# A transformer block on one core: the order of work at the joints of the transposed attention

## The reference, cut to what matters

```python
x = L0_attn_hidden_states                  # 2 x 2048 x 256, float32
x = x + 0.5 * ffn(layernorm(x))            # network 1
x = x + attention(layernorm(x))            # complex projections, softmax over 2048 keys
x = x + 0.5 * ffn(layernorm(x))            # network 2
# ffn(x) = fp4(silu(fp4(x) @ fp4(w_gate).T) * (fp4(x) @ fp4(w_up).T)) @ fp4(w_down).T
# fp4: blocks of 16 along the last axis, scale = max|block| / 6, values rounded to a grid of 8
# attention: the scores are the sum over a real and an imaginary part, one softmax for both
```

## Time and profile before

| | us |
|---|---|
| median of 3 runs | 1010.31 (1008.29 to 1010.52) |
| the profiled execution's own time | 1008.92 |
| its span, first to last instruction | 1007.1 |
| PE busy | 934.5 (93% of the span) |
| DVE, ACT, POOL busy | 709.0, 656.7, 505.5 |
| mean granted TensorE clock | 0.981 of full speed |

### The profile page before, as it was taken

The page is one execution under the profiler, slowest core; times in us unless marked ns, Lnnn a source line. Parts: engine busy times, 40 slices in busy tenths (PEclk is TensorE's granted clock), DMA queues, the critical chain, the costliest instruction groups (busy, mean ns, idle before and its releaser), DMA issues.

```text
span 1007.1 us, 18220 instructions
## 1 busy us (share of the span) xinstructions
PE 934.5 (93%) x6607; PEld 870.9 (86%) x6607; DVE 709.0 (70%) x1180; ACT 656.7 (65%) x1380; POOL 505.5 (50%) x593
## 2 busy tenths in 40 slices
PE   3799999999989489999989999999988999999997
PEld 2578888888889489999989999999977888888886
DVE  7889888888757436666555445555575889898996
ACT  5767877888755646666667566666674565555553
POOL 3456667665420074555555535555572565656552
PEclk9999999999999889999999999999999999999998
DMA  9000000000000000000000000000000000000001
GB/s 322 21 1 1 1 2 1 1 1 1 2 1 1 1 1 2 1 2 2 1 2 1 1 2 2 1 1 2 1 2 1 1 22 22 21 22 22 22 1 42
DMA packets 11560, 13.94 MB, mean 14 GB/s; under 512 B 848, under 2 KB 10576, under 8 KB 11472
## 3 DMA queue, kind: packets, MB, share of 16 engines
q1 hardware_dynamic: 11472, 12.79, 3.8%
HBM read 8.59 MB, written 4.19 MB: 13 GB/s over the span
## 4 chain that ended last, share of the span: by engine, by line
PE 65%; DVE 17%; POOL 7%; ACT 5%; issue 4%; DMA 0%; DVEq 0%; SPq 0%; ACTq 0%; POOLq 0%
PE bank L1711 18%; PE bank L1496 14%; POOL zq L487 6%; PE bank L1401 5%; DVE grid L696 3%; DVE amax L668 3%; PE bank_b L1505 3%; DVE rounded L690 3%; PE bank L1759 3%; PE bank_b L1763 3%; PE bank_b L1759 3%; PE bank L1763 3%; PE bank_b L1761 3%; PE bank L1761 3%; DVE z L657 2%
## 5 line engine op out<-in xcount | busy, mean ns | idle before, releaser
L525 POOL TENSOR_TENSOR p_lo<-s_buf,p_hi 128x512 fp32r<-128x512 f32 x128 | 165.0, 1293 | 176.4 <-ACT p_hi L1305 163.5
L487 POOL TENSOR_TENSOR zq<-grid,s_neg 128x64 f32<-128x64 f32 (+2 forms) x188 | 178.0, 971 | 60.3 <-DVE grid L696 50.9
L1496 PE MATMUL bank<-w_hi,T_hi 128*128 128x512 f32 (+1 forms) x384 | 150.1, 391 | 0.7 <-ACT T_lo L1148 0.7
L1711 PE MATMUL bank<-q_hi,k_hi 128*128 128x256 f32 x512 | 145.2, 284 | 1.8 <-DVE q_lo L824 1.8
L1711 PE MATMUL bank<-q_lo,k_hi 128*128 128x256 f32 x512 | 144.9, 283 | 0.0
L1711 PE MATMUL bank<-q_hi,k_lo 128*128 128x256 f32 x512 | 144.8, 283 | 0.0
L1496 PE MATMUL bank<-w_hi,T_lo 128*128 128x512 f32 (+1 forms) x384 | 144.5, 376 | 0.0
L1496 PE MATMUL bank<-w_lo,T_hi 128*128 128x512 f32 (+1 forms) x384 | 144.1, 375 | 0.0
L1290 ACT ACTIVATE s_buf<-bank 128x512 f32<-128x512 f32 x128 | 76.3, 596 | 99.0 <-PE bank L1711 99.0
L849 DVE TENSOR_TENSOR top<-bank,top 128x512 f32<-128x512 f32 x96 | 66.3, 691 | 75.9 <-ACT s_buf L1290 75.9
L1505 PE MATMUL bank_b<-wd_hl,T_hi 128*128 128x256 f32 x744 | 100.0, 283 | 3.0 <-ACT T_hi L1150 2.9
(11 more groups left out here) (202 smaller groups left out, 2541.1 us busy)
## 6 DMA issues: line engine op xcount, KB each, us to landing
out<-x SPq DMA_DIRECT2D x7, 512.0 KB, 2.9
x<-in_L_attn_hidden_states SPq DMA_DIRECT2D x3, 1024.0 KB, 13.9
x<-in_L_attn_hidden_states SPq DMA_DIRECT2D x2, 512.0 KB, 7.9
wraw<-in_L_ffn_w_down SPq DMA_DIRECT2D x1, 704.0 KB, 8.5
wraw<-in_L_ffn_w_gate SPq DMA_DIRECT2D x1, 640.0 KB, 4.6
wraw<-in_L_ffn_w_up SPq DMA_DIRECT2D x1, 640.0 KB, 6.6
wq_s<-in_L_attn_Wq SPq DMA_DIRECT2D x1, 512.0 KB, 8.1
wk_s<-in_L_attn_Wk SPq DMA_DIRECT2D x1, 512.0 KB, 9.5
```

Source lines behind the costliest of these rows:

```text
L487: last = nc.gpsimd.tensor_tensor(out=blocks(zq[:, to:to + hi - lo]), in0=blocks(grid[:, lo:hi]), in1=spread(s_neg[:, par, lo // BLOCK:hi / ...
L525: nc.gpsimd.tensor_tensor(out=p_lo[:, n % 2, 2 * c:2 * c + 2, :], in0=score_buf(n, c), in1=p_hi[:, 2 * c:2 * c + 2, :].bitcast(F32), op=AL ...
L1496: last = nc.tensor.matmul(gu[:, lo:hi], lhsT=T[:, par, HK + kd, :], rhs=w[:, kd, lo:hi], start=n == 0, stop=n == len(terms) - 1)
L1711: last = nc.tensor.matmul(score_bank(c)[:, a, :], lhsT=kk[:, kd, t], rhs=q[:, n % 2, kd, :], start=i == 0 and a == 0, stop=i == len(terms) ...
```

## The change

- **Query bias.** PE does `query_bias` in the first ramp, behind the first transposes of Wo, and ACT's two copies of it stand behind `chain_upper(-3)`. The sum moves to another bank.
- **Exp table.** The load moves from between `evacuate(0, 7)` and `evacuate(1, 0)` to the end of network 1, ahead of `bias_rows`.
- **First group.** On POOL `output_std(7)` moves behind the eight `p_lower(0, c)`. On DVE the shift runs one chunk behind the maximum instead of three.
- **Change of batch.** PE's first transpose of new keys waits for six evacuated chunks instead of eight. `queries(8)` moves from chunk 5 to chunk 2 on PE, and with it its two halves on ACT and DVE; the halves of the keys move one place; ACT's `new_statistics(5)` goes behind the eight exponentials.
- **Last group and ramp.** The first tile of group 15 is summed in `top_bank` instead of `bank_a`. The wait for `x_att` = 32 leaves ACT, and PE has it ahead of `transpose_chain(1, 0)`. On PE the transposes and the gate products of the ramp move forward by one to three chunks of weighted values; on POOL the first `quantised` moves ahead of the last two `p_lower`; on DVE `finish(14)` moves ahead of the scales of the second tile, `finish(15)` behind step -1; on ACT `chain_upper(-4)` goes ahead, and the statistics of group 15 go from step -1 to step 2.

The diff, cut to its core:

```diff
@@ banks
+        def out_bank(n, a):
+            return top_bank if n == NQ - 1 and a == 0 else value_banks[a]
-        bq_sum = bank4[:, 0, 0:1 + KD]
+        bq_sum = bank2[:, 0, 0:1 + KD]
@@ gpsimd
-                    if f == 0 and c % 4 == 1 and c >= 5:
+                    if f == 0 and c % 4 == 1 and 5 <= c < NT:
                         output_std((c - 5) // 4)
...
                 for c in range(CH):
                     p_lower(n - 1, c)
+                if n == 1:
+                    output_std(NG * B - 1)
...
             for c in range(CH):
+                if c == CH - 2:
+                    second_ffn(-5, 1)
                 p_lower(NQ - 1, c)
@@ vector
             running_top(1, 2)
+            shifted(0, 0)
+            shifted(0, 1)
             for c in range(3, CH):
-                shifted(0, c - 3)
                 running_top(1, c)
-            for c in range(CH - 3, CH):
-                shifted(0, c)
+                shifted(0, c - 1)
+            shifted(0, CH - 1)
...
-                if n == NQ - 1:
-                    second_blocks(-5, 1)
+            to_grid(-4)
             finish(NQ - 2)
+            scales(-3, 1)
+            scaled(-3)
             second_blocks(-4, 0)
             second_blocks(-3, 1)
             second_product(0)
             second_ffn(-2, 0)
+            second_ffn(-1, 1)
             finish(NQ - 1)
-            ffn_rounds(second_ffn, -1)
+            ffn_rounds(second_ffn, 0)
@@ scalar
-                    if f and c == -1:
-                        act.wait_ge(x_att, NT)
-                    if f and c == -1:
+                    if f and c == 2:
                         new_statistics(NQ - 1)
                     if extra and c == NT - 1:
+                        nc.scalar.activation(warm[:], mhalf[:, 0:1], ACT.Exp)
                         bias_rows()
...
-                new_statistics(n - 2)
+                if n != HQ - 1:
+                    new_statistics(n - 2)
...
+                if n == HQ - 1:
+                    new_statistics(n - 2)
@@ tensor
+                    if f and c == 0:
+                        pe.wait_ge(x_att, NT)
                     transpose_chain(f, c)
...
                 if n == HQ - 1:
-                    pe.wait_ge(evac_done, CH * (n + 1))
-                    pe.wait_ge(top_done, tops(n, CH - 1))
+                    pe.wait_ge(evac_done, CH * n + 6)
+                    pe.wait_ge(top_done, tops(n, 5))
                     transpose_keys(1, 0)
...
-            weighted_values(n, 0)
             pe.wait_ge(diff_done, CH * NQ)
             transpose_chain(1, -4)
+            weighted_values(n, 0)
+            chain_lower(1, -4, 0)
             weighted_values(n, 1)
-            chain_lower(1, -4, 0)
-            weighted_values(n, 2)
             pe.wait_ge(lo_done, number_lo(1, -4))
             gate_up(0, ((0, 512), (512, 1024), (1024, G))).then_inc(gu_done, 1)
             transpose_chain(1, -3)
+            weighted_values(n, 2)
+            chain_lower(1, -3, 1)
             weighted_values(n, 3)
             weighted_values(n, 4)
-            chain_lower(1, -3, 1)
+            ramp(-2, 0)
             weighted_values(n, 5)
             weighted_values(n, 6)
-            ramp(-2, 0)
+            ramp(-1, 1)
             weighted_values(n, 7)
-            rounds(1, -1)
+            rounds(1, 0)
```

57 lines of the change are left out of this document (28 added, 29 removed).

## The result

| | before | after |
|---|---|---|
| median | 1009.38 (4 runs: 1008.29 to 1010.52) | 984.06 (4 runs: 983.04 to 985.51) |
| the profiled execution's own time | 1008.92 | 983.04 |
| its span | 1007.1 | 981.3 |
| PE busy | 934.5 (93%) | 930.5 (95%) |
| mean granted clock | 0.981 | 0.991 |

The ratio is 0.975, with a 95% interval of 0.9734 to 0.9767: 25.3 us faster by the medians, 25.9 between the two profiled executions. The prediction was 984.0 (980 to 991.5).

What follows compares the result with a forecast made beforehand. The prediction took PE's own work to bound the steady attention, leaving waits and half clock at the joints. Its terms, -2.8 - 17.6 - 2.2 - 2.7 = -25.3 us, gave 983.6 from the profiled run, 985.0 from the median; forecast 984 (980 to 991.5).

Steps and rivals of the forecast that it cites:

- Query bias, -2.8: First ramp and attention's start: moving the one-column passes lets PE start earlier and keep its clock, -2.8 us in sum.
- The block: Attention's start: without the 24 one-column passes PE goes on at 292.4, -1.7 us.
- The clock: Attention's start: half clock from 294.90 to 298.20, put down to the one-column passes, would go: -1.1 us, or 0.
- The table load ahead of `bias_rows`: Attention's start: the Exp load delays ACT's chain by 1.3 us, but costs PE nothing, with +1.3 as other end.
- First group, -17.6: First attention group: shorter ACT rounds, POOL's wait gone and full clock together give -17.6 us.
- (a): First group: earlier shifts on DVE cut ACT's round from 3.13 to 1.78 us, `transpose_top(1)` comes 5.6 us earlier.
- (b): First group: POOL's lower parts no longer wait for tile 31's statistics, so the wait ahead of `weighted_values(0, 0)` goes: -9.6 us.
- (c): First group: half clock behind the two idle times goes, as about 2.5 us of wait remain: -2.4 us, other end 0.
- Change of batch, -2.2: Change of batch: PE's two waits give -1.0 and -1.8 us, ACT's late statistics cost +0.6; bounds -2.8 and 0.
- Last group and ramp, -2.7: Last group to network 2: -2.9 up to tile 0, -1.1 of clock behind it, +1.3 for late statistics; bounds +2 and -4.5.
- so the half clock stays as it was: Last group: PE idles 3.9 us ahead of the first transposes, so the clock loss there was taken as unchanged.
- that rival: First group: DVE's shift and maximum wait for POOL's parts, the round stays long at 4.0 us; 992 us, 8%.

Runs made afterwards that it cites:

- e10_narrow24: Changed kernel with 24 one-column passes (twelve matmuls) put at the attention's start, behind the transposes of the keys: 986.7 us.
- e5_wide: Changed kernel with 22 matmuls of 256 columns put at the attention's start, behind the transposes of the keys: 984.2 us.
- e1_pool: Kernel before with only POOL's first-group edit, `output_std(7)` behind the eight `p_lower(0, c)`: 1000.6 us against 1010.5.
- e2_dve: Kernel before with only DVE's first-group edit, the shift one chunk behind the maximum instead of three: 1001.5 us against 1010.5.
- e12_ramp: `e8_zq4_up` with `chain_rest(-4)` ahead of ACT's Silu table load and PE's last weighted values of group 15 spread between ramp stages: 980.3 us.
- e3_both: Kernel before with POOL's and DVE's first-group edits together, nothing else of the change: 994.2 us against 1010.5.
- e6_split: Changed kernel with the statistics of group 15 split: tile 30 in step 2, tile 31 in step 3 of network 2: 983.9 us.
- e7_zq4: Changed kernel with network 2's first quantised on POOL moved two lower parts earlier, ahead of `p_lower(15, 4)`: 982.5 us.
- e8_zq4_up: `e7_zq4` with ACT's `chain_upper(-4)` also moved, between the upper parts of chunks 6 and 7: 981.8 us.
- e4_narrow: Changed kernel with 12 one-column passes (six matmuls) put at the attention's start, behind the transposes of the keys: 983.0 us.
- e11_evac: Changed kernel with ACT's evacuations of chunks 6 and 7 of group 1 ahead of the exponentials of chunks 3 and 4: 983.8 us.
- e13_all: `e12_ramp` plus `e11_evac`'s order, a later `weighted_values(15, 7)`, statistics of tiles 28 to 31 in steps 0 to 3, DVE's last group-0 shift later: 974.6 us.

## Why the prediction was right

Point by point, by its own steps.

*Query bias, -2.8: right in sum, its two sizes off.* The start gained 2.8 us (2.4 at `scores(0, 0)`, with the first gate products 0.4 us later in the span before anything changed had run). The block is 1.2, not 1.7: `queries(0)` does begin 1.7 us earlier, but 0.4 us go again at the second transposes of keys, for which see the table load below. The clock is 1.6, not 1.1; I had counted matmuls only to 298.20. That the fall hangs on the one-column passes was a guess from one row. `e10_narrow24` against `e5_wide` supports it, but `e1_pool` and `e2_dve` have the passes and no fall: the 1.6 us are what the profiled run of the kernel before had to give, not what every run has. In the first ramp the passes cost nothing, since they lie in the old wait, which ends at 39.15 where it ended at 38.97:

```profile
39.15 0.58 PE L1543 MATMUL bank<-T_hi,neg_ident 128*128 128x256 f32 x1 [2.28 <-ACT T_hi L1152]
```

They saved nothing either: in the first ramp the ledger has 1.6 to 3.0 us in the four kernels with the passes at their old place, and 1.6 to 2.9 in the others (4.8 in `e12_ramp`). So the lower bound of -1.5, the clock kept in this gap, did not come.

The table load ahead of `bias_rows` was put at nothing, and no wait of PE at that place names ACT. But it did cost, by way of DVE:

```profile
293.02 1.06 DVE L647 SCALAR_TENSOR_TENSOR st_junk<-x,nmean,rk_row 128x256 f32<-128x256 f32 x1 [0.27 <-ACT bias_row L1075]
...
298.35 0.47 PE L1700 MATMUL bank<-nv,k_hi 128*128 128x256 f32 x2 [0.18 <-DVE v_hl L842]
```

DVE waited for ACT's row, and then its first statistic ran beside POOL's `bias_row` (293.07, 0.74 us) and took 1.06 us. Before, where POOL was through by then, it was:

```profile
292.28 0.48 DVE L639 SCALAR_TENSOR_TENSOR st_junk<-x,nmean,rk_row 128x256 f32<-128x256 f32 x1
```

From there DVE had no idle time until `v_hl` was done, and PE waited for that at 298.35. From the second transposes of keys to the product behind them PE took 298.35 - 297.13 = 1.22 us, where it took 0.79 before. So the term was about 0.4 us, within its bound of +1.3, but not nothing. This is read from the trace; no run has the load moved alone.

*First group, -17.6: right, -17.8.* (a) -5.8 against -5.6: the round is 1.67 us, a little under my 1.78, since I had left out how far ACT's instructions overlap. (b) -9.6, as read. (c) -2.4, as worked out, but in part by luck. I argued that waits of 1.46 and 1.82 us were not followed by a fall and took 2.5 us for the same kind. Of the nine kernels profiled here with a wait of 2.4 us ahead of `transpose_top(1)` and none behind it, six show a fall behind it, with 1.5 to 1.7 us lost (`e3_both`, `e6_split`, `e7_zq4`, `e8_zq4_up`, `e10_narrow24`, `e12_ramp`), three none (the changed kernel, `e4_narrow`, `e5_wide`). The profiled run of the changed kernel is its fastest; its other runs, up to 985.5, may hold the fall, which can't be seen, as they have no trace. In the profiled run of `e3_both`, with the same wait, only 0.85 of the 2.4 us came.

*Change of batch, -2.2: -2.8.* The wait for `queries_lower(8)` went whole. ACT's late statistics gave 0.3 us back (`scores(8, 0..7)` take 11.9 us instead of 11.6), where I took 0.6; and PE waits 0.54 us for the last maximum, as in the prediction. No experiment was made on this part alone.

*Last group and ramp, -2.7: right in sum by terms that cancel.* The first transposes came 0.3 us later than I had them. The step "so the half clock stays as it was" failed in this trace: behind 4.06 us of idle time 2.7 us are lost, where it was 1.4 before, so that up to tile 0 the gain is 1.6 and not 2.9. Here too the outcome varies. Six profiled kernels have this wait (4.04 to 4.09 us). Three lose 2.7 to 3.0 us behind it (the changed kernel, `e4_narrow`, `e11_evac`), three 1.7 (`e5_wide`, `e6_split`, `e10_narrow24`), and with 1.7 the gain up to tile 0 is 2.5 or 2.6 us. `e7_zq4`, with 1.42 us of idle time there, shows what cutting the wait is worth: 2.8 us against the changed kernel, 1.8 or 1.9 against those three. From tile 0 to 1 it is -1.4 (-1.1 predicted). The late Silu cost what was predicted: 8.60 us between the transposes of tiles 3 and 4 against 7.2, shown by `e6_split`. And 1.0 us came where I had no term: tiles 29 to 31 take 10.1 us instead of 11.1, since the fall of the clock at the very end costs 1.7 us instead of 2.8. That is luck and no gain of the change: `e7_zq4` and `e13_all`, with the same code there, lose 2.8.

*The rivals.* The round did not stay long. The mechanism behind that rival, DVE held up beside POOL, is real (`e11_evac`, and the statistic at 293.02 above), but it struck neither the shift of a chunk nor the maximum, each of which reads a bank and one SBUF tile. Network 2 kept its rhythm of 7.0 and 7.3 us a tile.

All in all the waits of each joint went as forecast, within 0.4 us of their terms. That the median, 984.06, meets the 984 so closely is luck: at four places (294, 337, 722 and the very end) the falls of the clock differ from kernel to kernel by 1.0 to 1.7 us, and here these differences happen to cancel.

Open is what decides whether the clock falls behind 2.4 us of idle time or behind the one-column passes, and how much is lost behind 4 us of idle time and at the end.

## What to carry to other kernels

Read a joint by the idle time of the engine that bounds the steady part, and look for a cause of its own for each wait; then ask in what order the *other* engines do their work there, since most of the gains here are orders of ACT, DVE and POOL. Follow a wait back more than one step: the table load of ACT cost PE 0.4 us though every wait named DVE. Price a wait with what the clock loses behind it: about 4.06 us idle cost another 1.7 to 3.0, a single wait of 1.4 us nothing. Of two waits close together, 0.90 and 1.43 us did cost (`e12_ramp`), 1.42 and 2.04 did not (`e7_zq4`). Where a single change is worth less than such a fall, as in `e6_split`, the place in the trace tells more than the median.

## What the runs showed of the hardware

- Twenty-four passes of one column, without a gap, were followed by half clock like idle time in three of five profiled kernels (the one before, `e3_both` and `e10_narrow24`, 0.66 on average from 294 to 299 us in the last) and not in two (`e1_pool`, `e2_dve`). As long a row of 256-column matmuls was not, nor were twelve such passes, in one profiled kernel each.
- Two instructions of DVE on one column, with all operands in SBUF, took 2.32 us beside an unbroken row of POOL's subtractions on SBUF and 0.35 us in a pause of it; in the first case each ended within 0.02 us of the end of one of POOL's parts. DVE's shift of 512 columns from a bank kept its 0.68 us beside them.
- The same work does not always have its falls of the clock at the same places. The stretch from `transpose_top(15)` to tile 0, which `e1_pool` and `e2_dve` leave as it was, took 50.7 and 50.8 us against 48.6, with 3.9 us lost in the eleven us after 734 and 737 against 1.4 in the same place before. The runs of one kernel differ too: those of the kernel before have mean granted clocks of 0.975 to 0.983 and times of 1006.1 to 1011.8 us.
